# Edge sums of a graph layer as two rounded products of the high and low parts of the weighed rows

## What is computed

```
h = (xn @ W).reshape(N, HEADS, HEAD_DIM)          # 8 heads of 32
e = leaky_relu(a_src[src] + a_dst[dst], 0.2)
ee = exp(e - segment_max(e, dst)[dst])
denom = segment_sum(ee, dst)
alpha = ee / denom[dst]
msg = h[src] * alpha[:, :, None]
agg = segment_sum(msg, dst)                       # the edge sums
out = layer_norm(agg + xn @ W_res + bias)
ff = gelu_tanh(out @ ffn_w1 + b1) @ ffn_w2 + b2   # "node" work below
```

## Time and profile before

| | us |
|---|---|
| median of 3 runs | 3497.78 (3495.64 to 3499.82) |
| the profiled execution, its own time | 3506.43 |
| its span, first to last instruction | 3504.4 |
| PE busy | 2954.3 (84%) |
| DVE busy | 2148.3 (61%) |
| POOL busy | 1668.5 (48%) |
| ACT busy | 1289.7 (37%) |

### The profile page before, as it was taken

The page is one execution under the profiler, slowest core; times in us unless marked ns, Lnnn a source line. Parts: engine busy times, 40 slices in busy tenths (PEclk is TensorE's granted clock), DMA queues, the critical chain, the costliest instruction groups (busy, mean ns, idle before and its releaser), DMA issues.

```text
span 3504.4 us, 50076 instructions
## 1 busy us (share of the span) xinstructions
PE 2954.3 (84%) x17241; PEld 2574.9 (73%) x17241; DVE 2148.3 (61%) x5400; ACT 1289.7 (37%) x2496; POOL 1668.5 (48%) x1651
## 2 busy tenths in 40 slices
PE   6378888888988744757999989999999999999998
PEld 5347776777877744746888878788887878888786
DVE  9835555554655447546666676667666676666644
ACT  1002332332332422401444444444354544445554
POOL 4177777777777302267543444434443444443000
PEclk9979899998999956868999999999999999999999
DMA  9343333333333102565655555546455454545333
GB/s 304 96 123 103 102 103 103 103 103 103 103 103 103 46 7 76 177 170 144 206 181 161 181 177 159 170 153 187 157 172 176 155 183 152 182 151 176 126 109 121
DMA packets 259786, 490.91 MB, mean 140 GB/s; under 512 B 73341, under 2 KB 164991, under 8 KB 259523
## 3 DMA queue, kind: packets, MB, share of 16 engines
q1 hardware_dynamic: 181475, 272.65, 23.7%
q0 software_dynamic: 75168, 211.78, 20.9%
q10 hardware_dynamic: 2880, 3.15, 0.3%
HBM read 441.32 MB, written 46.10 MB: 139 GB/s over the span
## 4 chain that ended last, share of the span: by engine, by line
PE 41%; DVE 7%; issue 2%; ACT 2%; POOL 2%; DMA 1%; SPq 0%; DVEq 0%; POOLq 0%; ACTq 0%
PE PB L109 27%; PE PB L1907 8%; POOL G L1878 2%; PE PB L1932 2%; PE PB L1920 2%; DVE H2l L2369 1%; ACT TFm L2135 1%; DVE WG L2220 1%; DMA RI<-resd 1%; DVE H1l L2369 1%; PE PB L1967 1%; DVE XR L2381 0%; DVE OT L2194 0%; DVE XR L2361 0%; PE PB L1942 0%
## 5 line engine op out<-in xcount | busy, mean ns | idle before, releaser
L1878 POOL DMA_INDIRECT G<-tab,SRCL x784 | 809.3, 1032 | 971.2 <-DVE WG L2220 755.4
L638 POOL DMA_INDIRECT G<-tab,SRCL x782 | 769.2, 984 | 311.9 <-issue 298.8
L2135 ACT ACTIVATE TFm<-PB,BIA,SCL 128x512 f32<-128x512 f32 (+1 forms) x416 | 313.4, 753 | 636.6 <-PE PB L109 631.5
L1907 PE MATMUL PB<-WG,OR 128*128 128x264 f32 x1568 | 433.7, 424 | 8.6 <-DVE WG L2220 6.5
L658 PE MATMUL PB<-G,OR 128*128 128x257 f32 x782 | 270.9, 430 | 144.0 <-DMA G<-tab,SRCL 124.2
L1907 PEld LDWEIGHTS PB<-WG,OR 128*128 128x128 f32 x1568 | 314.9, 209 | 63.4 <-issue 10.0
L109 PE MATMUL PB<-MW,H2h 128*128 128x256 f32 x1568 | 308.2, 293 | 33.8 <-DVE H2l L2369 33.4
L109 PE MATMUL PB<-H1h,MW 128*128 128x512 f32 (+1 forms) x832 | 315.3, 423 | 19.1 <-DVE H1l L2369 17.9
L109 PE MATMUL PB<-YTMh,MW 128*128 128x512 f32 (+1 forms) x832 | 297.2, 400 | 0.0
L109 PEld LDWEIGHTS PB<-MW,H2h 128*128 128x128 f32 x1568 | 249.6, 191 | 50.6 <-DVE H2l L2369 37.7
L658 PEld LDWEIGHTS PB<-G,OR 128*128 128x128 f32 x782 | 135.0, 207 | 197.8 <-DMA G<-tab,SRCL 171.6
(11 more groups left out here) (335 smaller groups left out, 7335.5 us busy)
## 6 DMA issues: line engine op xcount, KB each, us to landing
MW<-msplit SPq DMA_DIRECT2D x312, 512.0 KB, 3.5
ROW<-relrow SPq DMA_DIRECT2D x196, 128.0 KB, 3.8
G<-tab,SRCL POOLq DMA_INDIRECT x1566, 2.8
msplit<-MWS SPq DMA_DIRECT2D x24, 512.0 KB, 3.7
tab<-ACC SPq DMA_DIRECT2D x7, 896.0 KB, 5.5
resd<-RSG SPq DMA_DIRECT2D x49, 128.0 KB, 1.8
RI<-resd SPq DMA_DIRECT2D x49, 128.0 KB, 3.2
AR<-tab SPq DMA_DIRECT2D x49, 128.0 KB, 3.4
```

The lines of the kernel that those rows point to most:

```text
L638: po.indirect_dma_start(b.G[:, u % RU, q, 0:256], None, c.tab0, bass.IndirectOffsetOnAxis(ap=c.SRCL[:, 2 * u + q:2 * u + q + 1].bitcast(U3 ...
L1878: po.indirect_dma_start(b.G[:, j % RP, u, :], None, c.tab1, bass.IndirectOffsetOnAxis(ap=c.SRCL[:, 4 * j + u:4 * j + u + 1].bitcast(U32), ...
L1907: ins = pe.matmul(PB[2][:, 0:264], b.OR2[:, j % 3, u, :].bitcast(F32), b.WG[:, j % 2, u, :], start=(first and u == 0), stop=(last and u == 3))
L2135: a.activation(b.TM[:, m, 0:n], PB[of][:, 0:n], ACT.Relu, bias=b.BIA[:, l, q:q + 1], scale=b.SCL[:, l, q:q + 1]).then_inc(relu, 1)
```

## The change

- `WG` becomes two tiles, `WGh` and `WGl`, both rounded fp32. DVE makes the weights into the gathered slot `G` itself and multiplies the rows in place. A new ACT instruction copies the 128x1056 weighed numbers to `WGh` (rounded), and a new DVE step, `low`, subtracts it and writes `WGl`.
- PE's sum of a unit is 4 times `OR` by `WGh` and `OR` by `WGl`, 8 rounded products of 128x264, in place of 4 plain ones of two instructions.
- The slot of `G` is given back to POOL after `low`, which stands in the plan one unit later than `weigh`.
- The plan's edge list is reordered and has new costs: onehot comes ahead, then low of the unit before, weight, and the sum last.
- For the room: `OR` has 2 slots for 3, `ROW` 3 for 4, `AR` (node rows) 10 for 11, `MW` 6 for 7. Each is requested one step of its own later accordingly.

```
-RQ = 7
+RQ = 6
-RA = 11
-RO = 4
+RA = 10
+RO = 3
...
         if i < NJ:
             put(("factors", i), 0.6)
+            put(("onehot", i), 0.7)
         if i:
-            put(("sum", i - 1), 1.7)
-            if i % 3 == 0 or i == NJ:
-                w = (i - 1) // 3
-                put(("evac", w), 0.3)
-                waiting.extend(ready_after(w))
+            put(("low", i - 1), 1.2)
         if i < NJ:
-            put(("onehot", i), 0.7)
...
             put(("weight", i), 0.4)
+        if i:
+            put(("sum", i - 1), 1.2)
+            if i % 3 == 0 or i == NJ:
+                w = (i - 1) // 3
+                put(("evac", w), 0.3)
+                waiting.extend(ready_after(w))
...
-    b.WG = sb("WG", [P, 2, 4, 264])
-    b.OR2 = sb("OR2", [P, 3, 4, P], F32R)
+    b.WG = [sb("WGh", [P, 2, 4, 264], F32R), sb("WGl", [P, 2, 4, 264], F32R)]
+    b.OR2 = sb("OR2", [P, 2, 4, P], F32R)
...
-                    ins = pe.matmul(PB[2][:, 0:264], b.OR2[:, j % 3, u, :].bitcast(F32), b.WG[:, j % 2, u, :],
-                                    start=(first and u == 0), stop=(last and u == 3))
+                    pe.matmul(PB[2][:, 0:264], b.OR2[:, j % 2, u, :], b.WG[0][:, j % 2, u, :],
+                              start=(first and u == 0), stop=False)
+                    ins = pe.matmul(PB[2][:, 0:264], b.OR2[:, j % 2, u, :], b.WG[1][:, j % 2, u, :],
+                                    start=False, stop=(last and u == 3))
...
+        elif step == "weigh":
+            j, = x
+            on.wait_ge(S.product, j + 1)
+            if j >= 2:
+                on.wait_ge(S.edge_mm, j - 1)
+            a.copy(b.WG[0][:, j % 2, :, :], b.G[:, j % RP, :, 0:264]).then_inc(S.high, 1)
...
-        if j >= 3:
-            on.wait_ge(S.edge_mm, j - 2)
+        if j >= 2:
+            on.wait_ge(S.edge_mm, j - 1)
...
+        elif step == "low":
+            j, = x
+            on.wait_ge(S.high, j + 1)
+            on.wait_ge(S.product, j + 1)
+            v.tensor_tensor(b.WG[1][:, j % 2, :, :], b.G[:, j % RP, :, 0:264], b.WG[0][:, j % 2, :, :].bitcast(F32),
+                            ALU.subtract).then_inc(S.weighed, 1)
```

More of the change, by code:

```diff
@@ L1384, in row_in @@
 def row_in(S, j):
-    return (S.row_in0, S.row_in1, S.row_in2, S.row_in3)[j % RO]
+    return (S.row_in0, S.row_in1, S.row_in2)[j % RO]
 def unit_of(group):
@@ L1406, in piece_in @@
 def piece_in(S, q):
-    return (S.mw_in0, S.mw_in1, S.mw_in2, S.mw_in3, S.mw_in4, S.mw_in5, S.mw_in6)[q % RQ]
+    return (S.mw_in0, S.mw_in1, S.mw_in2, S.mw_in3, S.mw_in4, S.mw_in5)[q % RQ]
 def edge_stream(fast):
@@ L1421, in put @@
             t = tok[1]
-            if t + 3 < NT:
-                out.append((("fetch_self", t + 3), 0.0))
+            if t + 2 < NT:
+                out.append((("fetch_self", t + 2), 0.0))
             if t + 1 < NT:
@@ L1428, in put @@
                 out, g = [], g + 1
-    for t in range(3):
+    for t in range(2):
         put(("fetch_self", t), 0.0)
@@ L2183, in onehot @@
     def onehot(j):
-        if j >= 3:
-            on.wait_ge(S.edge_mm, j - 2)
-        v.tensor_tensor(b.OR2[:, j % 3, :, :], c.iotaf[:, :].unsqueeze(1).to_broadcast([P, 4, P]),
+        if j >= 2:
+            on.wait_ge(S.edge_mm, j - 1)
+        v.tensor_tensor(b.OR2[:, j % 2, :, :], c.iotaf[:, :].unsqueeze(1).to_broadcast([P, 4, P]),
                         c.REL[:, 4 * j:4 * j + 4].unsqueeze(2).to_broadcast([P, 4, P]), ALU.is_equal).then_inc(S.onehot, 1)
@@ L2211, in last_dve @@
             on.wait_ge(S.factor, j + 1)
-            if j >= 2:
-                on.wait_ge(S.edge_mm, j - 1)
-            own.mark(v.tensor_tensor(b.WG[:, q, :, 256:264], b.E1[:, q, :, 0:8], b.E1[:, q, :, 8:16], ALU.max))
+            own.mark(v.tensor_tensor(b.G[:, j % RP, :, 256:264], b.E1[:, q, :, 0:8], b.E1[:, q, :, 8:16], ALU.max))
             weights_done = own.n
@@ L2217, in last_dve @@
             j, = x
-            q = j % 2
             on.wait_ge(own.sem, weights_done)
-            v.tensor_tensor(b.WG[:, q, :, 0:256].rearrange("p u (h d) -> p u h d", h=8),
-                            b.G[:, j % RP, :, 0:256].rearrange("p u (h d) -> p u h d", h=8),
-                            b.WG[:, q, :, 256:264].unsqueeze(3).to_broadcast([P, 4, 8, 32]),
-                            ALU.mult).then_inc(S.weighed, 1)
+            row = b.G[:, j % RP, :, 0:256].rearrange("p u (h d) -> p u h d", h=8)
+            v.tensor_tensor(row, row, b.G[:, j % RP, :, 256:264].unsqueeze(3).to_broadcast([P, 4, 8, 32]),
+                            ALU.mult).then_inc(S.product, 1)
+        elif step == "low":
[4 more added lines that the diff above has]
+                            ALU.subtract).then_inc(S.weighed, 1)
         elif step == "self":
@@ L2398, in last_layers @@
 def last_layers(nc, c, A, out):
-    S = named(nc, c, "last", "dve consts g_in0 g_in1 g_in2 g_in3 g_in4 g_in5 nd_in0 nd_in1 nd_in2 nd_in3 nd_in4 nd_in5 nd_in6 nd_in7 row_in0 row_in1 row_in2 row_in3 onehot rowhot "
-                             "nd_mm factor weighed edge_mm evac shift tile_mm sums self_in0 self_in1 self_in2 self_in3 "
+    S = named(nc, c, "last", "dve consts g_in0 g_in1 g_in2 g_in3 g_in4 g_in5 nd_in0 nd_in1 nd_in2 nd_in3 nd_in4 nd_in5 nd_in6 nd_in7 row_in0 row_in1 row_in2 onehot rowhot "
+                             "nd_mm factor product high weighed edge_mm evac shift tile_mm sums self_in0 self_in1 self_in2 self_in3 "
                              "weighed_self x_in0 x_in1 res_in0 res_in1 res_add var std rows rows_t rows_out rows_hi rows_lo "
@@ L2403, in last_layers @@
                              "xrows_hi xrows_lo logit_mm logit centred expd share share_t share_out bo_mm bo_add "
-                             "mw_in0 mw_in1 mw_in2 mw_in3 mw_in4 mw_in5 mw_in6 h1_mm h2_mm h1_relu h2_relu h1_hi h2_hi h1_lo "
+                             "mw_in0 mw_in1 mw_in2 mw_in3 mw_in4 mw_in5 h1_mm h2_mm h1_relu h2_relu h1_hi h2_hi h1_lo "
                              "h2_lo out_mm out_add shared stored0 stored1 stored2 stored_end")
```

## The result

The changed kernel took 3535.07 us (median of 4 runs, 3528.53 to 3539.89), beside 3498.8 us for the kernel before on the same chip: a ratio of 1.010, 95% interval 1.0075 to 1.0125. It is slower by 36 us where I forecast faster by 26. The time lies inside the range, at its far end (3540). Rival 2 comes nearest: slower, with a new wait of DVE for the cast.

The account below looks back on a forecast made before the run. PE was taken to bound A, DVE B and latency C; -35 us from 1700 us on, +8 at the start and +1 for the chain's start made -26 us: 3480 us profiled, 3472 us median, range 3405 to 3540.

Parts of the forecast that it names:

- Rival 2: Over 176 units DVE becomes the bound, with a new wait for ACT's cast: 53 us more, 3550 us; chance 0.26.
- A: Stretch with feed-forward steps, 90 us, 9 units, bound by PE: PE saves 8.1 us, net -7.6 us.
- B: Stretch where node rows are normalised, 30 us, 5 units, bound by DVE: grows by 4.6 us (3.3 to 5.9).
- C: Stretch where rows are prepared for the experts, 20 us, 2 units, bound by latency: 0, bounds -1.8 and +2.8 us.
- Rival 1: PE stays the bound nearly everywhere from 1700 to 3230 us: 105 us less, 3393 us; chance 0.2.
- crowded spots: In the feed-forward stretches, 0.5 us of PE's 8.1 us saving is given back, leaving -7.6 us.
- the sign I named (over 95%): Sign of being right: in the feed-forward stretches PE still over 95% busy, a unit shorter by some 0.85 us.
- 35 us of the forecast: From 1700 to 3289 us, 11.8 groups of four node tiles at -3.0 us each: -35 us.
- upper bound of 5.9: Where node rows are normalised: growth in us if none of DVE's free time could be used, 5 units at 1.18.
- half clock: At 1.2 GHz PE's saving of 0.90 us a unit would about double; left out, the granted clock being 0.96.
- a fall below 0.94: Sign on PE's granted clock: below 0.94, the saving of 0.90 us a unit was priced wrongly.
- the start: 1500 to 1700 us: low lengthens gathers through the port DVE and GpSimd share; +8 us, bounds 0 and 18.

Follow-up runs that it names:

- rings and order: Kernel before with the smaller rings and the new order and costs of the edge list, plain products, no low: 3493.01 us, 0.9982 of the kernel before.
- kernel without low: Changed kernel with the cast but without DVE's subtraction, the high product run twice (also called no low): 3395.17 us, 0.9699 of the kernel before.
- rings: Kernel before with only the smaller rings (MW, AR, ROW, OR), plain products, old order: 3509.12 us, 1.0037 of the kernel before.
- none: As rings and order, but plain products read from G, held until PE is done, and plain sums priced at 1.7: 1.0051 of the kernel before.
- first 60: Same code as none, but products of parts in units 0 to 59 only: 1.0082 of the kernel before.
- from 60 on: Same code as none, but products of parts in all units from 60 on: 1.0036 of the kernel before.
- series 2: Second series of runs, on chips 2, 9 and 11: the kernel before takes 3740 us instead of 3498, the changed kernel 3773.06 us (1.0079).

## Why the prediction was wrong

**What held.** Eight products from first start to next work:

```profile
2443.01 0.28 PE L1909 MATMUL PB<-WGh,OR 128*128 128x264 f32 x1
...
2443.86 0.29 PE L1911 MATMUL PB<-WGl,OR 128*128 128x264 f32 x1
...
2443.99 0.40 PE L109 MATMUL PB<-MW,H2h 128*128 128x256 f32 x2
```

0.98 us, predicted 0.97. Low and cast had the predicted length. That PE's saving counts in A and hardly elsewhere was right: against rings and order, the products alone save 7.8 us in A (8.1 predicted), 0.8 in B and 0.7 in C. C fell by 0.6 (0 predicted), of which the order gave 2.5 and low took 2.6. Rival 1 falls by the same rows: PE is at 88%.

**The step that failed: "I give back 0.5 us for crowded spots. Net -7.6 us."** A became 4.0 us shorter, not 7.6. PE was still at 95% there (81.11 of 85 us), so the sign I named (over 95%) held only just and was too coarse: what mattered was the 5% that it had lost, from 100%. The kernel without low has A at 83.5 us, so low costs 3.1 us in A, six times what I gave back. My ground was that 17% of DVE's time was free and PE had 4 us in hand. An average of free time says nothing of the moment: DVE's free time had been for a large part its waits for a cast of ACT that itself waits for PE (HT9h 193.1 us), and these were used up. Over the eight groups PE is idle in A for 1.4 us before, 2.0 without low and 3.8 after. Of the 1.8 us that low adds, 0.7 are waits for H1l and H2l, 0.5 for low itself and 0.5 for HT9l; the rest of the 3.1 us is PE busy for longer. With A at -4.0, B at +5.0 and C at -0.6 a group is +0.4 us instead of -3.0, which takes away the 35 us of the forecast. Those 35 were 31 to begin with: from 1700 to 3289 us before there are 165 units, 10.3 groups of 16 and not 11.8, because a group takes 152.8 us in the mean and not 135.

**B: the number was luck.** B grew by 5.0 us in the mean, near the 4.6 forecast, but the group of the earlier trace rows is not typical. One B like it and the one after it, before:

```profile
2374.70:2407.00 32.30, 27.36 (x143) 23.45 (x143) 29.24 (x74) 12.20 (x19) 19.82 (x19) 0.96 0.78 244
2514.90:2562.70 47.80, 43.05 (x204) 35.41 (x205) 34.85 (x93) 16.58 (x27) 20.43 (x20) 0.88 0.60 194
```

and the same units after:

```profile
2401.30:2443.30 42.00, 30.87 (x149) 26.79 (x149) 35.17 (x78) 18.23 (x26) 20.92 (x17) 0.80 0.56 178
2547.00:2596.70 49.70, 41.87 (x218) 35.06 (x216) 40.99 (x98) 22.78 (x32) 25.95 (x22) 0.86 0.59 183
```

Three of the eight groups have the short B, with DVE busy for 90%; five have one of 47 to 50 us, with DVE at 72 to 80%. The short ones grew by 10.4 us in the mean, beyond my upper bound of 5.9, the long ones by 1.7. I had said that DVE bounds B and would be busy for 95% or more; it is at 84%, and either the load or the chain taken away brings B down (table). Against the kernel without low, low costs 6.5 us in B, more than the 5.9 us that it adds to DVE's time.

**The clock, a term left out.** I had set the half clock aside, since the granted clock was 0.96, and had named a fall below 0.94 as a sign of a wrong price. It fell to 0.93. The length of the products was right at full clock, but PE's busy time in the last stage fell by 87 us (1830 to 1743), not by the 146 us of the kernel without low.

**The second miss: the start, +9 us.** At unit 18 the kernel was 13 us late, at unit 35 17, at unit 59 36. I had put all of it on gathers. They were not the cause: the mean gather from 1505 to 1700 us took 1138 ns (1126 before), and DVE's waits for gathered rows fell from 45.5 us to 14.4 from 1505 to 1742 us. The kernel without low has the same gathers and is at unit 59 after 427 us, 50 less than after, so low costs 0.85 us a unit there, against 12.1 / 16 = 0.76 in a steady group. The waits in that view after are of the chain:

```profile
ACT WGh L2074 <- DVE G L2228: 85.9, 21, 19.3
PE PB L1909 <- DVE WGl L2234: 48.4, 23, 7.5
```

My working had A's and B's cost of low only from 1700 us on, and before it only a port. More than half of the miss (19 of 36 us) lies in units 35 to 59, where I expected a gain already. Of load and chain, neither taken away alone gives back much in the first units (at most 17 us).

**The third: the end.** From unit 195 to the last instruction it took 231 us, 221 before. Rings and order alone have 228, so 7 of the 10 us come with them. It goes with the price of the sum in the plan: where the last units are priced at 1.7 it is 219 to 221 us (before, rings, none, first 60), where at 1.2 it is 226 to 232 (rings and order, no low, after, from 60 on). A part of it is won just before, since units 187 to 195 take 93 to 95 us in the first four and 85 to 92 in the others. I had said that nothing changes there.

**The sum by place** (36 to unit 59, -6 from 59 to 187, -6 from 187 to 195, +10 behind it, -1 for an earlier unit 0) is +33 us, the difference of the profiled spans. Rival 2 forecast 3550 us by another sum: it had +53 us as steady cost, and in fact the steady part came out even and the start made the loss. It had the kind of waits right, and not their place, nor that DVE would stay at 79%.

Left open: why series 2 takes 240 us more, why low later in the plan lengthens B, how much of the loss is the clock's, and what of load and chain holds the first 59 units.

## What to carry to other kernels

When work moves from an engine at 94% to one at 67%, price what is added twice, as time on the second engine and as a link in the chain, and weigh it against the waits by which that engine now trails the first: here taking away the one gave 62 us, the other 54, and both 140, against 98 us saved. The stretch in which the first engine was all but 100% busy was the only place where its saving counted in full (7.8 of 8.1 us); to change only the units there was better than to change all from unit 60 on (0.9956 against 1.0037), though not shown better than to change none. Read more than one group before taking it for the mean, and count the first units by themselves.
